# Writing the degree term of each gate tile into its PSUM bank before the matmuls, in place of adding it behind them

## What is computed

```python
Af = A.astype(float32); AfT = Af.T; state = x
for _ in range(5):
    s_in = state @ in_W.T + in_b;  s_out = state @ out_W.T + out_b
    a_in = Af @ s_in;              a_out = AfT @ s_out
    a = concatenate([a_in, a_out, state])
    r = sigmoid(a @ r_W.T + r_b);  z = sigmoid(a @ z_W.T + z_b)
    h_hat = tanh(concatenate([a_in, a_out, r * state]) @ h_W.T + h_b)
    state = (1 - z) * state + z * h_hat
out = layernorm(x + tanh(state @ o1_W.T + o1_b) @ o2_W.T + o2_b)
```

## Time and profile before

| | us |
|---|---|
| three timed runs | 1097.23, 1095.56, 1097.20 |
| median | 1097.2 |
| span of the profiled execution, first to last instruction | 1094.1 |
| TensorE busy | 1070.0 |
| VectorE busy | 582.4 |
| ScalarE busy | 249.8 |

### The profile page before, as it was taken

One profiled execution on the slowest core, in us unless ns is written; L12 is line 12 of the kernel. 1 busy time (PEld: TensorE's weight loads), 2 busy tenths in 40 slices (PEclk: granted clock), 3 DMA queues, 4 the chain that ended last, 5 costly groups with the idle time before them and its releaser, 6 DMA issues.

```text
span 1094.1 us, 12578 instructions
## 1 busy us (share of the span) xinstructions
PE 1070.0 (98%) x5160; PEld 497.1 (45%) x5160; DVE 582.4 (53%) x1024; ACT 249.8 (23%) x314; POOL 22.4 (2%) x27
## 2 busy tenths in 40 slices
PE   6999999999999999999999999999999999999994
PEld 3444444444444444444444444444444444444442
DVE  5944478854443536271726262635445363747466
ACT  3666322221211111121112112112121121111111
POOL 0300000020000000000000000000000000101000
PEclk9999999999999999999999999999999999999998
DMA  9989100010000000000000000000000000101000
GB/s 339 398 309 398 67 1 1 1 39 1 1 1 1 1 1 1 2 1 1 1 1 1 1 1 2 1 1 1 1 1 1 1 1 1 39 1 39 1 20 19
DMA packets 13638, 46.30 MB, mean 42 GB/s; under 512 B 1168, under 2 KB 7952, under 8 KB 9488
## 3 DMA queue, kind: packets, MB, share of 16 engines
q1 hardware_dynamic: 13584, 45.49, 10.9%
HBM read 43.39 MB, written 2.10 MB: 42 GB/s over the span
## 4 chain that ended last, share of the span: by engine, by line
PE 95%; DVE 2%; DMA 1%; SPq 1%; ACT 1%; issue 0%; DVEq 0%
PE bank L646 50%; PE bank L724 42%; PE bank L737 1%; DMA tmp<-in_adj 1%; PE bank L766 1%; PE bank L748 1%; SPq L196 0%; DVE deg_words L477 0%; ACT tmp L307 0%; DVE tmp L502 0%; ACT a L270 0%; DVE pq_words L418 0%; SPq L193 0%; SPq L192 0%; DVE pq_words L574 0%
## 5 line engine op out<-in xcount | busy, mean ns | idle before, releaser
L724 PE MATMUL bank<-pq_words,w 128*128 128x512 f16 x1440 | 327.6, 379 | 0.0
L646 PE MATMUL bank<-a,state_n 128*128 128x512 fp8e4 x1280 | 280.8, 379 | 3.3 <-ACT a L270 3.3
L646 PE MATMUL bank<-at_words,state_n 128*128 128x512 fp8e4 x1280 | 282.0, 379 | 0.2
L418 DVE SCALAR_TENSOR_TENSOR pq_words<-bank,pq_words 128x512 f16<-128x512 f32 x80 | 55.2, 691 | 350.2 <-ACT pq_words L297 328.1
L724 PEld LDWEIGHTS bank<-pq_words,w 128*128 128x128 f16 x1440 | 140.8, 98 | 168.3
L646 PEld LDWEIGHTS bank<-at_words,state_n 128*128 128x128 f16 x1280 | 124.6, 98 | 149.4 <-issue 1.1
L646 PEld LDWEIGHTS bank<-a,state_n 128*128 128x128 f16 x1280 | 124.3, 98 | 150.0 <-issue 3.9
L307 ACT ACTIVATE tmp<-tmp,bias_sb,scal 128x512 f32<-128x512 f32 x120 | 97.3, 813 | 394.4 <-DVE tmp L502 394.4
L724 PE MATMUL bank<-split_t,w 128*128 128x512 f16 x480 | 116.7, 379 | 0.6 <-DVE deg_words L477 0.6
L502 DVE TENSOR_TENSOR tmp<-bank,tmp 128x512 f32<-128x512 f32 x120 | 82.5, 689 | 57.4 <-PE bank L724 56.6
L297 ACT ACTIVATE pq_words<-bank 128x512 f16<-128x512 f32 x64 | 38.2, 597 | 315.0 <-PE bank L646 315.0
(11 more groups left out here) (90 smaller groups left out, 383.2 us busy)
## 6 DMA issues: line engine op xcount, KB each, us to landing
tmp<-in_adj SPq DMA_DIRECT2D x16, 1024.0 KB, 6.8
tmp<-in_adj_t SPq DMA_DIRECT2D x16, 1024.0 KB, 6.9
pq_words<-in_gate_w SPq DMA_DIRECT2D x6, 384.0 KB, 6.1
at_words<-in_x SPq DMA_DIRECT2D x4, 512.0 KB, 8.4
state_t<-in_x_t SPq DMA_DIRECT2D x4, 512.0 KB, 7.7
pq_words<-in_x SPq DMA_DIRECT2D x4, 512.0 KB, 4.2
out<-pq_words SPq DMA_DIRECT2D x8, 256.0 KB, 2.3
deg_words<-in_io_w SPq DMA_DIRECT2D x4, 128.0 KB, 4.0
```

What stands on the lines that cost most here:

```text
L418: return nc.vector.scalar_tensor_tensor(pq[:, c, q, 1, :], src[:, :], PSC, pq[:, c, q, 0, :], ALU.mult, ALU.subtract).then_inc(done, 1)
L646: return nc.tensor.matmul(dst[:, :], state_n[:, j, part, feat(f)], adj8[:, j, cols(c)], start=j == 0 and part == 0, stop=j == JT - 1 and p ...
L724: last = nc.tensor.matmul(dst[:, :], w16[:, k, wp, feat(gi)], rhs, start=i == 0 and (wp, xp) == PASSES[0], stop=i == KT - 1 and (wp, xp) = ...
```

## The change

The degree term no longer goes through `pre`. ScalarE writes its first product into the gate tile's bank (`seed`), VectorE adds the second in the bank (`degree_part`), TensorE starts the tile on `s_c1`, with no matmul that clears the bank (`start=False`), and ScalarE's activation reads the bank. `pre`, `gate_pre` and `s_pre` are gone. The seeds of tiles 3 to 5 are issued behind the activations of tiles 0 to 2, those of the next chunk's tiles 0 to 2 behind the activations of tiles 3 to 5. In the last step, chunks 1 to 3, the head uses the banks first: there ScalarE seeds tiles 0 to 2 behind the high half of product 2, and VectorE's parts stand between the layer norm and the low half of product 3. Two waits are new: an activation of r or z waits for the update of the chunk before (`s_new`), and `keep_part` for the split of r * state (`s_rsl`). In `head_out`, where two results share a bank, only the first clears it now.

```diff
@@ scalar
             def gate_act(n, gi):
                 dst = (r_buf, z_buf, h_buf)[gi // FT]
-                act.wait_ge(s_pre, GT * n + gi + 1)
-                nc.scalar.activation(dst[:, gi % FT, :], pre[:, gi % 3, :], ACT.Tanh if gi >= 2 * FT else ACT.Sigmoid,
+                act.wait_ge(s_gate, GT * n + gi + 1)
+                if gi < 2 * FT and not (isinstance(n, int) and n == 0):
+                    act.wait_ge(s_new, FT * n + gi % FT - 1)
+                nc.scalar.activation(dst[:, gi % FT, :], gate_bank[gi % 3][:, :],
+                                     ACT.Tanh if gi >= 2 * FT else ACT.Sigmoid,
                                      bias=bias_sb[:, 4 + gi:5 + gi], scale=UG).then_inc(s_act, 1)
+            def seed(n, c, gi, head=None):
+                if not (isinstance(n, int) and n == 0 and gi < 3):
+                    act.wait_ge(s_act, GT * n + gi - 2)
+                if head is not None and gi < 2:
+                    act.wait_ge(s_hid, FT * head + gi + 1)
+                if head is not None and gi == 2:
+                    act.wait_ge(s_y, JC * head + 2)
+                nc.scalar.activation(gate_bank[gi % 3][:, :], deg[:, 0, cols(c)], ACT.Identity,
+                                     scale=vdeg[:, 0, gi:gi + 1]).then_inc(s_c0, 1)
+
+            def gates(n, c, between=False, last=False):
+                for gi in range(GT):
+                    gate_act(n, gi)
+                    if between and gi in (3, 4):
+                        nat_out(n - 1, c - 1, gi - 3, True)
+                    if gi < 3:
+                        seed(n, c, gi + 3)
+                    elif not last:
+                        seed(n + 1, (c + 1) % CH, gi - 3)
...
                     pq_hi(n, 2)
+                    if c > 0 and last:
+                        for gi in range(3):
+                            seed(n, c, gi, head=c - 1)
                     pq_hi(n, 3)
...
             act.wait_ge(s_bias, 16)
+            act.wait_ge(s_deg, 2 * CH)
+            for gi in range(3):
+                seed(0, 0, gi)
@@ vector
             def degree_part(n, c, gi):
-                g = GT * n + gi
-                slot = pre[:, gi % 3, :]
-                if not (isinstance(n, int) and n == 0 and gi < 3):
-                    dve.wait_ge(s_act, g - 2)
-                nc.vector.tensor_scalar(slot, deg[:, 0, cols(c)], vdeg[:, 0, gi:gi + 1], None, ALU.mult) \
-                    .then_inc(s_c0, 1)
-                dve.wait_ge(s_c0, g + 1)
+                slot = gate_bank[gi % 3][:, :]
+                dve.wait_ge(s_c0, GT * n + gi + 1)
                 nc.vector.scalar_tensor_tensor(slot, deg[:, 1, cols(c)], vdeg[:, 1, gi:gi + 1], slot,
                                                ALU.mult, ALU.add).then_inc(s_c1, 1)
-            def gate_pre(n, gi):
-                g = GT * n + gi
-                slot = pre[:, gi % 3, :]
-                dve.wait_ge(s_c1, g + 1)
-                dve.wait_ge(s_gate, g + 1)
-                nc.vector.tensor_tensor(slot, gate_bank[gi % 3][:, :], slot, ALU.add).then_inc(s_pre, 1)
...
             def keep_part(n, c, f):
                 dve.wait_ge(s_act, GT * n + 2 + f + 1)
+                dve.wait_ge(s_rsl, FT * n + f + 1)
...
-            def gates(n, c):
-                for f in range(FT):
-                    degree_part(n, c, f)
-                for f in range(FT):
-                    gate_pre(n, f)
+            def gates(n, c, last=False):
                 for f in range(FT):
                     reset_part(n, c, f)
-                for f in range(FT):
-                    degree_part(n, c, FT + f)
-                    gate_pre(n, FT + f)
+                    degree_part(n, c, 3 + f)
+                degree_part(n, c, 5)
                 for f in range(FT):
                     keep_part(n, c, f)
+                if not last:
+                    for f in range(FT):
+                        degree_part(n + 1, (c + 1) % CH, f)
                 for f in range(FT):
-                    degree_part(n, c, 2 * FT + f)
-                for f in range(FT):
-                    gate_pre(n, 2 * FT + f)
                     update(n, c, f)
+                if not last:
+                    degree_part(n + 1, (c + 1) % CH, 2)
...
                     if last and c > 0:
                         residual(c - 1)
                         layer_norm(c - 1)
+                    if last and c > 0:
+                        for gi in range(3):
+                            degree_part(n, c, gi)
                     pq_lo(n, 3)
...
+            for gi in range(3):
+                degree_part(0, 0, gi)
@@ tensor
-                        last = nc.tensor.matmul(dst[:, :], w16[:, k, wp, feat(gi)], rhs,
-                                                start=i == 0 and (wp, xp) == PASSES[0],
-                                                stop=i == KT - 1 and (wp, xp) == PASSES[-1])
+                        last = nc.tensor.matmul(dst[:, :], w16[:, k, wp, feat(gi)], rhs, start=False,
+                                                stop=i == KT - 1 and (wp, xp) == PASSES[-1],
+                                                skip_group_check=True)
...
                             last = nc.tensor.matmul(head_rows(c, j), hid16[:, k, xp, j * P:(j + 1) * P],
                                                     o16[:, k, wp, D:2 * D],
-                                                    start=k == 0 and (wp, xp) == PASSES[0],
+                                                    start=k == 0 and (wp, xp) == PASSES[0]
+                                                    and (c == CH - 1 or j % 2 == 0),
...
                 for gi in range(GT):
-                    if isinstance(n, int) and n == 0 and gi < 3:
-                        pe.wait_ge(s_deg, CH + gi + 1)
-                    else:
-                        pe.wait_ge(s_pre, GT * n + gi - 2)
-                    if last_step and c > 0 and gi < 2:
-                        pe.wait_ge(s_hid, FT * (c - 1) + gi + 1)
-                    if last_step and c > 0 and gi == 2:
-                        pe.wait_ge(s_y, JC * c - 2)
+                    pe.wait_ge(s_c1, GT * n + gi + 1)
                     gate_tile(n, c, gi, slot, ready)
```

More of the change, by code:

```diff
@@ L103, in gnn_program @@
         stage = tmp[:, :].bitcast(I32).rearrange("p (s n) -> p s n", s=STG)
-        pre = tmp[:, 0:3 * CW].rearrange("p (b n) -> p b n", b=3)
         r_buf = tmp[:, 3 * CW:5 * CW].rearrange("p (f n) -> p f n", f=FT)
@@ L150, in gnn_program @@
         s_c0, s_c1 = sem("s_c0"), sem("s_c1")
-        s_pre = sem("s_pre")
         s_act = sem("s_act")
@@ L305, in gate_act @@
                 dst = (r_buf, z_buf, h_buf)[gi // FT]
-                act.wait_ge(s_pre, GT * n + gi + 1)
-                nc.scalar.activation(dst[:, gi % FT, :], pre[:, gi % 3, :], ACT.Tanh if gi >= 2 * FT else ACT.Sigmoid,
-                                     bias=bias_sb[:, 4 + gi:5 + gi], scale=UG).then_inc(s_act, 1)
[L310 to L313, removed]
-                for f in range(FT):
[L315 to L318, removed]
+                act.wait_ge(s_gate, GT * n + gi + 1)
[3 more added lines that the diff above has]
+                                     ACT.Tanh if gi >= 2 * FT else ACT.Sigmoid,
+                                     bias=bias_sb[:, 4 + gi:5 + gi], scale=UG).then_inc(s_act, 1)
+            def seed(n, c, gi, head=None):
[16 more added lines that the diff above has]
+                        seed(n + 1, (c + 1) % CH, gi - 3)
             def head_act(c):
@@ L340, in step @@
                     pq_hi(n, 2)
+                    if c > 0 and last:
+                        for gi in range(3):
+                            seed(n, c, gi, head=c - 1)
                     pq_hi(n, 3)
-                    gates(n, c)
+                    gates(n, c, last=last)
                 if last:
@@ L617, in step @@
                         nc.vector.tensor_copy(state_n[:, 0:JH, :, :], next_n).then_inc(s_cur, 1)
-                    gates(n, c)
+                    gates(n, c, last)
                 if last:
@@ L767, in head_out, with gates @@
                                                     o16[:, k, wp, D:2 * D],
-                                                    start=k == 0 and (wp, xp) == PASSES[0],
-                                                    stop=k == FT - 1 and (wp, xp) == PASSES[-1])
+                                                    start=k == 0 and (wp, xp) == PASSES[0]
+                                                    and (c == CH - 1 or j % 2 == 0),
+                                                    stop=k == FT - 1 and (wp, xp) == PASSES[-1],
+                                                    skip_group_check=True)
                         if k == FT - 1 and (c == CH - 1 or j % 2):
                             last.then_inc(s_o2, 1)
-            def gates(n, c, slot, ready, last_step=False, between=None):
+            def gates(n, c, slot, ready, between=None):
```

(11 more changed lines are left out.)

## The result

| | before | changed |
|---|---|---|
| median, us | 1097.12 (4 runs) | 1101.78 (4 runs, 1100.31 to 1103.08) |
| ratio | | 1.0045, interval 1.0031 to 1.006 |
| span of the profiled execution | 1094.1 | 1101.3 (its own time 1103.08) |
| mean granted clock | 0.997 | 0.991 |

The change costs 4.7 us by the medians. That is outside the forecast range (1096.5 to 1101.5) by 0.3 and on the side of rival A. The profiled execution is the slowest of the four; its span is 7.2 over the one before, and those 7.2 can be laid out piece by piece.

The account below looks back on a forecast made before the run. TensorE was taken to bound the kernel, so only its idle places count: 3.2 + 0 + 0.3 - 2.1 = +1.4 us on the median 1097.2 gives 1098.6. The range was 1096.5 to 1101.5.

Parts of the forecast that it names:

- rival A: Ahead of the first gate tile: a 3.9 us gap halves the clock, 1.5 us more, +2.9 in all, 1100.1; chance 0.28.
- What bounds it: From step 0 through the loop: TensorE has no gap, so VectorE and ScalarE savings there are worth nothing unless something becomes late.
- step 2: Inside step 0 and the looped steps: seeds and VectorE's parts arrive in time, at least 2.7 us of cover; costs nothing.
- Step 1: Before the first gate tile: it must wait for a seeded bank, so it starts 3.2 us later (3.0 to 3.5).
- Step 3: Last step, chunks 1 to 3: VectorE's part behind layer norm starts TensorE 0.1 us late each, 0.3 in all.
- Step 4: After the last gate tile: activation reads the bank itself and VectorE is free, so the second update starts 2.1 us earlier.
- The sum without the clock: Whole kernel, all four steps at full clock: 3.2 + 0 + 0.3 - 2.1 = +1.4 us, between +0.8 and +2.65.

Follow-up runs that it names:

- experiment 6: Kernel before, changed with the first-gate-tile gap open, changed with it filled, changed without late places; other gaps filled by spare matmuls: 1095.41, 1099.37, 1096.98, 1093.85 us.
- experiment 2: Kernel before with added waits for VectorE's degree parts: first run, gate tiles 0 to 2, 1112.63 us; second run, very first tile only, 1104.16 us.
- 4: Changed kernel with one VectorE copy of the very last gate tile out of its bank ahead of its activation: 1102.29 us, run once.
- the wait on the first tile: Kernel before with one wait more, for VectorE's degree part at the very first gate tile only: 1104.16 us, ratio 1.0068.
- the open gap of 6: Changed kernel with gaps at the start and in the last head filled by spare matmuls, the one ahead of the first gate tile open: 1099.37 us.
- experiment 5: Changed kernel with first three gate tiles done as before, and last step's seeds and VectorE parts of tiles 0 and 1 ahead of layer norm: 1097.17 us.
- experiments 3: Changed kernel with each early seed issued when its own bank is free and VectorE's parts between the last degree casts: 1097.05 us, ratio 1.0001.
- experiment 1: Changed kernel with 18 spare matmuls ahead of the first gate tile, into a bank nobody reads: 1099.69 us, ratio 1.0024 to the kernel before.

## Why the prediction was wrong

The forecast (no change that can be told, 1098.6) was wrong: 4.7 us are clear of the 2.2 that it took as the least that can be told. Rival A, at 0.28, had the mechanism.

- **What bounds it, and step 2**: right. TensorE waits nowhere between the first and the last gate tile but for the 0.3 of the last step; 131 us less on VectorE gained nothing there.
- **Step 1, the late start**: right in place and close in size: +3.45 measured, 3.24 forecast, end 3.5. The seed was shorter than I took (691 against 770 ns), the hand-overs longer: 0.09 to ScalarE, some 0.1 to VectorE, 0.14 to TensorE, where I had 0.02 to 0.03 each. The two errors partly cancel.
- **Step 3**: 0.1 three times, as forecast. **Step 4**: -2.17 in the trace, forecast -2.1. The sum without the clock was +1.4; with every gap filled the medians give +1.57, and the pieces in those two traces 3.37 (a gap of 3.99 against 0.62) + 0.3 - 2.17 = 1.5, so this agreement is not luck.
- **The step that failed** is the sum's silence on what follows the gap of step 1: it lets the matmuls behind the gap run at full pace, and puts their delay at nothing. The runs show them at half clock, 2.4 us by the medians of experiment 6. I had the mechanism only as a rival, at 0.28, because one gap of 3.31 us in the trace had left the clock alone. In all five profiled executions that have this gap open (4.1 to 4.2 us: changed, experiments 2, 4, the wait on the first tile and the open gap of 6) the clock is low behind it. With a gap of that length it should have been the likeliest case.
- **Its price** was mis-sized: 1.5 by the 2.9 us that the clock took to fall at the end; measured 2.48 in the changed kernel's trace, between 1.7 and 2.9 in the other four. With 2.4 rival A says 1097.2 + 3.8 = 1101.0, inside the range.
- **The scatter**: I added the change to a median of three runs that lay 1.7 apart and took the scatter as noise. It is low clock in two other gaps. The medians differ by 4.66, and by 3.96 with those gaps filled; the 0.7 between them is what carried the time over the top of the range, but it is inside the interval of the four runs (3.4 to 6.6 us), so the last 0.3 us over the range are chance as far as the runs can tell.

What stays open: why experiment 5, with the start's gap as in the kernel before and the last head's as in the changed one, ran with a low mean clock in eleven of twelve executions, when the kernel before, with the same gap at the start, did so far less often (most at 0.996 or 0.997). Filling the gaps removes it; what decides in which execution the clock falls was not tried. The late store is open too.

## What to carry to other kernels

Work moved off an engine that isn't the bound is worth only what it frees at the places where the bounding engine stands still; read those places first, and count what the new work adds ahead of the first of them. When a change lengthens an idle stretch of TensorE to some microseconds, put the slower matmuls behind it into the sum, not among the rivals. Before comparing medians a few microseconds apart, look for other such gaps: filling them with spare matmuls made differences of 1.5 us readable.

## What the runs showed that I had not expected

- The same short gap gives both outcomes. At the start, gaps of 3.30, 3.66 and 2.52 us left the clock at 1.00 (kernel before, experiments 3 and 5), and gaps of 3.58, 2.85 and 3.68 us lowered it (changed kernel, experiment 4, and the first run of experiment 2), as did 4.36 and 4.60 (its second run and experiment 1).
- How long the clock stays low varies: behind a gap of 4.1 to 4.2 us the first gate tile took 5.6 us in two executions and 6.3, 6.4 and 6.8 in three, where it takes 3.9.
- Filling one gap of the kernel before changed its median by 0.1 us, filling all of them by 1.8.
- ScalarE writes 512 columns of 32 bits to PSUM in 691 ns with one pointer operand named in the code, and VectorE's multiply-add reads and writes PSUM in 752 ns, as long as in SBUF (751).
